# The first block's Silu through Tanh, one more VectorE operation per slice, and a new order of the instructions

## The reference

```python
qkv = jnp.einsum('bnd,ed->bne', x, W_qkv)               # x is layer-normed
attn = softmax(einsum('bnd,bmd->bnm', q * DIM**-0.5, k))
out = einsum('bnm,bmd->bnd', attn, v)
x = x + _layernorm(out)
# feed-forward on layernorm(x); _tlin(x, w, s) = (x @ w.T) * s, w is -1, 0 or 1
h = silu(_tlin(x, w1_w, w1_s)) * _tlin(x, w2_w, w2_s)   # 128 -> 512
h = gelu(_tlin(h, h1_w, h1_s))                          # 512 -> 512
h = gelu(_tlin(h, h2_w, h2_s))                          # 512 -> 512
x = x + _layernorm(_tlin(h, w3_w, w3_s))                # 512 -> 128
```

## Time and profile before

| what | us |
|---|---|
| median of 3 runs (129.56 to 130.08) | 129.98 |
| the profiled execution, its own time | 130.0 |
| its span, first to last instruction | 127.8 |
| PE busy | 122.6 |
| VectorE busy | 103.3 |
| ScalarE busy | 97.4 |
| table loads on ScalarE, up to 27 us: those at 0.75, 18.76, 23.35 and 25.69 | 4 x 1.28 |

### The profile page before, as it was taken

One profiled execution on the slowest core, in us unless ns is written; L12 is line 12 of the kernel. 1 busy time (PEld: TensorE's weight loads), 2 busy tenths in 40 slices (PEclk: granted clock), 3 DMA queues, 4 the chain that ended last, 5 costly groups with the idle time before them and its releaser, 6 DMA issues.

```text
span 127.8 us, 2356 instructions
## 1 busy us (share of the span) xinstructions
PE 122.6 (96%) x698; PEld 102.5 (80%) x698; DVE 103.3 (81%) x337; ACT 97.4 (76%) x182; POOL 27.9 (22%) x40
## 2 busy tenths in 40 slices
PE   7999999999999999999999999999999999999980
PEld 5585979989778988887889888888888788899970
DVE  0697789998898997888798998458999895695853
ACT  4248887987999739599899189799992996997520
POOL 3294220033300015230000054400001550000351
PEclk9999999999999999999999999999999999999999
DMA  4899999100000000010000000010000002000003
GB/s 106 250 308 379 381 375 373 33 5 3 0 0 5 0 5 0 3 41 0 0 5 0 0 5 0 16 68 0 8 0 0 0 5 82 0 5 0 0 29 100
DMA packets 5344, 8.28 MB, mean 65 GB/s; under 512 B 465, under 2 KB 2769, under 8 KB 5329
## 3 DMA queue, kind: packets, MB, share of 16 engines
q1 hardware_dynamic: 3840, 5.12, 12.6%
q0 software_dynamic: 1344, 2.88, 6.7%
q10 hardware_dynamic: 144, 0.07, 0.2%
HBM read 7.02 MB, written 1.05 MB: 63 GB/s over the span
## 4 chain that ended last, share of the span: by engine, by line
PE 84%; DVE 6%; DMA 3%; ACT 1%; SPq 1%; issue 1%; DVEq 0%; ACTq 0%
PE F L1181 22%; PE F L1187 22%; PE A L1090 5%; PE A L1058 5%; PE F L1130 5%; PE F L1137 5%; PE A L1187 3%; PE A L1181 3%; DMA xs<-x 3%; PE A L1041 3%; PE A L1074 2%; PE A L1029 2%; DVE xn_odd L653 2%; PE F L1210 1%; PE A L1222 1%
## 5 line engine op out<-in xcount | busy, mean ns | idle before, releaser
L319 POOL TENSOR_TENSOR rstd<-mv,minus_half 128x4 f32<-128x4 f32 (+1 forms) x19 | 17.7, 935 | 87.1 <-DVE mv L637 87.0
L1181 PE MATMUL F<-a_hi,h_hi 128*128 128x512 f32 (+1 forms) x152 | 35.5, 355 | 0.0
L630 DVE TENSOR_TENSOR a_lo<-act_full,a_hi 128x512 fp32r<-128x512 f32 (+1 forms) x52 | 30.6, 602 | 5.9 <-ACT act_full L432 5.2
L1187 PE MATMUL F<-a_lo,h_hi 128*128 128x512 f32 (+1 forms) x152 | 34.9, 352 | 0.0
L440 ACT ACTIVATE a_hi<-F,sc 128x512 fp32r<-128x512 f32 (+1 forms) x33 | 20.5, 632 | 12.2 <-PE F L1187 12.2
L1187 PEld LDWEIGHTS F<-a_lo,h_hi 128*128 128x128 f32 x152 | 25.7, 189 | 4.0
L1181 PEld LDWEIGHTS F<-a_hi,h_hi 128*128 128x128 f32 x152 | 25.2, 189 | 3.6 <-issue 0.2
L432 ACT ACTIVATE act_full<-F,sc 128x512 f32<-128x512 f32 (+1 forms) x38 | 23.1, 621 | 1.7 <-PE F L1187 1.7
L733 DVE SCALAR_TENSOR_TENSOR act_full<-F,sc,silu 128x512 f32<-128x512 f32 (+1 forms) x16 | 10.7, 676 | 1.0 <-ACT silu L421 0.8
L421 ACT ACTIVATE silu<-F,sc 128x512 f32<-128x512 f32 (+1 forms) x16 | 9.8, 633 | 1.1 <-PE F L1137 0.9
L1130 PE MATMUL F<-x2T_hi,w_hi 128*128 128x512 f32 (+1 forms) x32 | 10.3, 405 | 0.1
(11 more groups left out here) (158 smaller groups left out, 198.5 us busy)
## 6 DMA issues: line engine op xcount, KB each, us to landing
h_raw<-h SPq DMA_DIRECT2D x2, 1024.0 KB, 11.2
h_hi<-h POOLq DMA_DIRECT2D x2, 1024.0 KB, 12.1
xs<-x SPq DMA_DIRECT2D x3, 256.0 KB, 3.9
out<-outs SPq DMA_DIRECT2D x3, 256.0 KB, 2.1
w_raw<-w SPq DMA_DIRECT2D x1, 512.0 KB, 6.4
w_hi<-w POOLq DMA_DIRECT2D x1, 512.0 KB, 7.3
xs<-x SPq DMA_DIRECT2D x2, 128.0 KB, 8.9
w_raw<-w SPq DMA_DIRECT2D x1, 256.0 KB, 16.1
```

The source lines that it names most:

```text
L319: nc.gpsimd.tensor_tensor(rstd[:, ln, tiles(b)], mv[:, ln, tiles(b), 1], minus_half[:, 0:SIZES[b]], ALU.pow).then_inc(rstd_ready[ln], 1)
L630: nc.vector.tensor_tensor(dst, full, hi.bitcast(f32), ALU.subtract).then_inc(done, 1)
L1181: nc.tensor.matmul(out, terms[k][0], terms[k][2], start=(k == 0), stop=False)
L1187: last = [nc.tensor.matmul(out, terms[k][0], terms[k][3], start=False, stop=(k == KT - 1)) for out, terms in groups]
```

## The change

In block 0 alone (`BY_TANH = (0,)`) ScalarE computes t = tanh(w1_s/2 * u) where it computed Silu(w1_s * u), u being the first product in PSUM. VectorE then makes (t + 1) * u of it, in place in `silu1` (`one_and_tanh`, new, four calls of 128x256), and the gate multiplies with w1_s * w2_s / 2 in place of w2_s. The two new columns of scales, `half_w1` and `half_w12`, are made by two small VectorE instructions (`halves`). Tanh is in the table set that Exp uses.

One of the copies of block 1, `pT_copy(1, 0)`, goes from VectorE to ScalarE. The order of all engines' lists is new in many places; the numbers of instructions are otherwise as before, but for `keep_warm`, of which 6 of the 8 ahead of `x_transposes(1)` are gone, and the 2 ahead of `g_projection(0)` stand in their place.

```diff
+        half_w1, half_w12 = sb("half_w1", [P, KT]), sb("half_w12", [P, KT])
+        BY_TANH = (0,)
-        BY_DVE = ((0, 0, 0, 1, 1), (0, 0, 0, 1, 1), (0, 0, 0, 1, 1), (1, 1, 0, 1, 1, 1, 0, 1))
+        BY_DVE = ((0, 0, 0, 1, 1), (0, 0, 0, 1, 1), (0, 0, 0, 1, 1), (1, 0, 0, 1, 1, 1, 0, 1))
@@ silu
+                if b in BY_TANH:
+                    act.wait_ge(halves_ready, 2)
+                    nc.scalar.activation(silu1[:, o % 2, c], up_banks(b, o)[0][:, c], ACT.Tanh,
+                                         scale=half_w1[:, o:o + 1]).then_inc(silu_ready, 1)
+                    return
@@ vector engine
+            def halves():
+                dve.wait_ge(sc_loaded, 16)
+                nc.vector.tensor_scalar(half_w1[:, :], sc[:, S_W1:S_W1 + KT], 0.5, None, ALU.mult).then_inc(halves_ready, 1)
+                nc.vector.scalar_tensor_tensor(half_w12[:, :], sc[:, S_W1:S_W1 + KT], 0.5, sc[:, S_W2:S_W2 + KT],
+                                               ALU.mult, ALU.mult).then_inc(halves_ready, 1)
+            def one_and_tanh(b, o):
+                c = slice(0, width(b))
+                dve.wait_ge(silu_ready, KT * b + o + 1)
+                nc.vector.scalar_tensor_tensor(silu1[:, o % 2, c], silu1[:, o % 2, c], 1.0, up_banks(b, o)[0][:, c],
+                                               ALU.add, ALU.mult).then_inc(silu_product, 1)
@@ gate
+                if b in BY_TANH:
+                    dve.wait_ge(silu_product, KT * BY_TANH.index(b) + o + 1)
+                    dve.wait_ge(halves_ready, 2)
+                    w2_scale = half_w12[:, o:o + 1]
@@ order on the vector engine, first block
+            halves()
+            x2T_low(0)
             low_sum(3)
@@ order on the tensor engine, before x_transposes(1)
-            keep_warm(F[0], 8)
```

More of the change, by code:

```diff
@@ L534, in _ @@
             gelu_high(A2, 1, 1)
+            gelu_high(A2, 1, 2)
             gelu(A2, 1, 1)
-            gelu_high(A2, 1, 2)
             gelu(A2, 1, 2)
@@ L825, in _ @@
             x1_normalised(0)
+            halves()
+            x2T_low(0)
             low_sum(3)
-            x2T_low(0)
-            pT_copy(1, 0)
+            squared_sums(1)
             low_sum(4)
-            squared_sums(1)
+            one_and_tanh(0, 0)
+            one_and_tanh(0, 1)
             gate(0, 0)
@@ L833, in _ @@
             high(A1, 0, 0)
+            low_sum(5)
+            attention_out(1)
+            maxima(2, 0)
+            one_and_tanh(0, 2)
             high(A1, 0, 1)
             low(A1, 0, 0)
+            copy_flags(1)
             low(A1, 0, 1)
-            low_sum(5)
             gate(0, 2)
+            one_and_tanh(0, 3)
             high(A1, 0, 2)
-            maxima(2, 0)
+            gate(0, 3)
             low(A1, 0, 2)
-            attention_out(1)
-            gate(0, 3)
             high(A1, 0, 3)
-            copy_flags(1)
             low(A1, 0, 3)
@@ L854, in _ @@
             low(A3, 0, 0)
+            low(A3, 0, 1)
             x2T_low(1)
-            x_normalised(3)
             maxima(2, 1)
             pT_copy(2, 0)
-            low(A3, 0, 1)
+            low(A3, 0, 2)
             gate(1, 0)
             gate(1, 1)
-            low(A3, 0, 2)
             low(A3, 0, 3)
             high(A1, 1, 0)
+            x_normalised(3)
+            squared_sums(2)
             high(A1, 1, 1)
+            pT_copy(2, 1)
             low(A1, 1, 0)
-            pT_copy(2, 1)
-            squared_sums(2)
+            gate(1, 2)
             low(A1, 1, 1)
-            gate(1, 2)
             high(A1, 1, 2)
@@ L898, in _ @@
             low(A1, 2, 0)
-            low(A3, 1, 3)
             pT_copy(3, 0)
+            gate(2, 2)
             high(A1, 2, 1)
-            gate(2, 2)
             high(A1, 2, 2)
@@ L946, in _ @@
             y_shifts(2)
-            x1_normalised(4)
             low(A2, 3, 0)
             low(A2, 3, 1)
+            x1_normalised(4)
+            x2T_low(4)
             low(A2, 3, 2)
-            x2T_low(4)
-            shift_x1(4)
             low(A2, 3, 3)
@@ L955, in _ @@
             gate(4, 1)
+            gate(4, 2)
             high(A1, 4, 0)
-            gate(4, 2)
+            high(A1, 4, 1)
+            low(A1, 4, 0)
+            shift_x1(4)
             gate(4, 3)
-            low(A1, 4, 0)
-            high(A1, 4, 1)
             high(A1, 4, 2)
             low(A1, 4, 1)
-            high(A3, 3, 0)
             high(A1, 4, 3)
             low(A1, 4, 2)
+            high(A3, 3, 0)
             low(A3, 3, 0)
@@ L1237, in _ @@
             x_transposes(0)
+            g_projection(0)
+            scores(0, 0)
+            v_projection(0)
+            w3_broadcast()
             keep_warm(A[0], 2)
-            g_projection(0)
-            v_projection(0)
-            scores(0, 0)
-            w3_broadcast()
-            keep_warm(F[0], 8)
             x_transposes(1)
@@ L1249, in _ @@
             scores(1, 0)
+            scores(1, 1)
             v_projection(1)
-            scores(1, 1)
+            sum_flags(0)
             g_projection(2)
-            sum_flags(0)
+            read_flag(0)
+            probs_transposes(1, 0)
+            x2_transposes(0)
             v_projection(2)
-            read_flag(0)
-            x2_transposes(0)
-            probs_transposes(1, 0)
-            probs_transposes(1, 1)
             up_high(0, 0)
@@ L1262, in _ @@
             up_low(0, 1)
+            probs_transposes(1, 1)
             attend(1, 0)
+            attend(1, 1)
+            scores(2, 0)
             up_high(0, 2)
@@ L1345, in _ @@
             up_low(3, 2)
+            up_high(3, 3)
+            probs_transposes(4, 0)
+            up_low(3, 3)
             end(A3, 2, (0,), 3)
-            probs_transposes(4, 0)
-            up_high(3, 3)
-            up_low(3, 3)
             attend(4, 0)
```

101 lines of the change are left out of this document (52 added, 49 removed).

## The result

| | median, us | runs |
|---|---|---|
| before, beside it | 129.77 | 129.36 to 130.08 |
| changed kernel | 132.88 | 131.01, 132.26, 133.5, 133.6 |

A forecast was written before the change was run, and what follows sets the result against it. PE bounds the kernel, busy for 122.6 of 127.8 us, with VectorE nearly full in block 0's gates. 130.0 us plus 1.5, less 0.25, less 0.25, gave 131.0; range 129.1 to 132.2.

The forecast's parts named there:

- ScalarE's loads at nothing: Block 0: removing two table loads, 2.57 us of ScalarE's time, gains nothing, with 0.5 us as the other end.
- The rival with ScalarE as pace-maker: Block 0: the loads held back Silus and exps, so the kernel gets faster, 128.5 us; chance 0.15.
- VectorE's price: Block 0's gates: VectorE gets net 1.6 us more work and starts 0.1 us later, so the last low ends at 28.5.
- So VectorE decides: Block 0's h1: PE is ready at 28.1, ahead of the last low, so its matmul starts 1.5 us later (1.1 to 1.9).
- VectorE's full stretch: Sign in block 0: VectorE busy without a gap from x2T_lo at about 18.9 to the last a_lo at about 28.5.
- PE's idle time at the flag's read: Sign around 17.3: PE stands from about 17.0 to 17.6; the 0.6 us are covered by later waits.
- the products' distance of 0.40: Sign in block 0: the four one_and_tanh on VectorE stand at distances of 0.40 us.
- The pair at 107.37: Sign near the end: this pair of matmuls stands at 108.6, showing what was given back until then.
- Given back from 34 to 43, 0.25: Later PE work: waits for a copy and for block 1's gates give 0.25 us back (0 to 0.6).
- Given back near the end, 0.25: At up_high(4, 2): shift_x1(4) moved behind the gates, and lows ahead of copies, give 0.25 us back (0 to 0.5).
- The other moves are each nothing: Rest of the kernel: other moves stand where PE has no wait; each costs nothing, or 0.1 us for one.
- The rival of the clock: Whole kernel: the clock case puts the time at 132.6 us; chance 0.08.

The follow-up runs named there:

- e11_before_no_product: e4_before_tanh without the four one_and_tanh, so the product by (tanh + 1) is left out; 129.72 us, ratio 0.9995.
- e3_warm_silu: e1_warm with Silu in block 0 again and without one_and_tanh and halves, the new orders kept; 134.74 us, ratio 1.0387.
- e1_warm: The changed kernel with keep_warm as before: 2 ahead of g_projection(0), 8 ahead of x_transposes(1); 131.63 us, ratio 1.014.
- e7_no_product: e1_warm without the four one_and_tanh of VectorE, so the product by (tanh + 1) is left out of block 0; 131.68 us, ratio 1.0142.
- e12_moved: e8_late_orders with Tanh and product, pT_copy(1, 0) on ScalarE and attention_out(1) behind block 0's last low; 131.93 us, ratio 1.0186.
- e4_before_tanh: The kernel before, in its orders, with Tanh, halves and the four one_and_tanh in block 0; 131.01 us, ratio 1.0094.
- e8_late_orders: The kernel before up to block 0's end, then the changed kernel's orders with x2T_low(4) behind low(A2, 3, 2); 129.65 us, ratio 0.9987.
- e6_warm_tail: e1_warm with x2T_low(4) put behind low(A2, 3, 2), as the kernel before has it; 131.0 us, ratio 1.0087.
- e5_warm_sum: e1_warm with low_sum(3) put back ahead of x2T_low(0), as the kernel before has it; 131.74 us, ratio 1.016.
- e2_cold: The kernel before with only its keep_warm matmuls cut as in the changed kernel; 130.24 us, ratio 1.0057.

## Why the prediction was right or wrong

**ScalarE's loads at nothing: right.** e11_before_no_product has them gone in the orders of before and pays no product: ratio 0.9995. The rival with ScalarE as pace-maker, 128.5 us, falls. In the changed kernel's trace no load stands between the Tanh at 24.99 and the exps at 25.79. e3_warm_silu shows the other side, four loads of 1.28 us where the calls alternate.

**VectorE's price: right in size, by luck.** I had the stretch from 18.87 to 28.5, 9.63 us; it is 9.56. The four products took 0.33 each, not 0.40, and about 0.2 is saved where the third and fourth gate are no longer followed at once by the `high` that reads them (0.39 and 0.40 to the next operation, 0.51 and 0.48 before). Against that, a wait of 0.44 that I hadn't seen stands between the two sums. The profile shows no releaser for it ("issue"). By the code a `low_sum` waits for the `low_sum` before it (`dve.wait_ge(low_by_dve, before)`), and the change takes away the copy that stood between them; but that alone isn't the cause, since in e3_warm_silu the same two sums, with the same tiny operation between them, start 0.80 us apart (19.44 and 20.24) and leave no gap, for 1.21 here. What makes the wait is open.

**"So VectorE decides": the step that failed, though its number held.** I put PE at 28.1, "just ahead of the last `low`", 9.23 behind `x2T_lo(0)`, and took the later of the two. They are a tie: in e1_warm the last `low` ends at 9.55, and PE, without idle time from `scores(2, 1)` on, comes to the matmul at 9.72. That is 0.49 later than I had it: `scores(2, 1)` starts 0.28 later (7.11 for 6.83), and from there PE takes 2.6 us, not 2.4. e7_no_product shows PE's own limit, where `low` is 0.80 earlier and PE only 0.28. The 1.5 us are right (9.72 for 8.30 is 1.42), but half of the cause is missing: `scores(2, 1)` ahead of `begin`, which puts 2.6 us of PE's work behind the exps instead of 1.26 (8.30 - 7.04); in e12_moved, with `begin` ahead again, it is 1.17 (8.88 - 7.71), though no run moved `begin` alone. Either cause by itself costs it nearly all: e4_before_tanh has only VectorE's (c 9.95), e7_no_product only PE's (c 9.44). Their prices don't add, and undoing one gives next to nothing back.

**What was to be seen.** Of the marks that the prediction named, ScalarE's one load, VectorE's full stretch (but for the 0.44) and PE's idle time at the flag's read (0.27 us for 0.6) and ahead of `scores(2, 1)` are there; the products' distance of 0.40 is not. `gelu_high(A2, 0, 0)` was to come at 28.9, 10.03 us behind `x2T_lo(0)`; it comes at 29.87, also 10.03 behind it. The pair at 107.37 was to stand at 108.6 and stands at 110.15, in e1_warm at 108.97: less was given back than forecast.

**Given back from 34 to 43, 0.25: the cause came, and most of it was lost again.** In e1_warm PE's delay against before is 1.19 us at block 1's first `up_high` (35.10 for 33.91) and 0.93 at `attend(2, 0)` (37.78 for 36.85), behind the copy that is no longer late: 0.26 as I said. But the next four matmuls, for which I named the wait for block 1's gates, are 1.13 late (39.07 for 37.94), and so is block 1's h1 (44.16 for 43.03). e8_late_orders shows the same two steps; e4_before_tanh, with the old orders, is 1.69, 1.70 and 1.69 late at these three places and gives nothing back. By the first matmuls of block 3's h2 (102.44 before) e1_warm is 1.01 late, e4_before_tanh 1.57.

**Given back near the end, 0.25: wrong in sign.** In e1_warm the delay grows from 1.01 to 1.48 us at the last matmul. I read the pair at 107.37, whose wait does go, and not what the same new order does to the queue ahead of it, `low(A2, 3, 2)` behind `x2T_low(4)`. e6_warm_tail shows its price, 0.53 us in the trace. This term, 0.25 less forecast and 0.5 more measured, is about what e1_warm's 131.63 lies above the forecast.

**"The other moves are each nothing": wrong. The clock: its time met in one execution, its term in none.** The rival of the clock, 132.6 us, to which I gave 0.08, was an estimate of mine, 1.6 us above the forecast, and no run shows that term; what the profiled execution, 132.26, shows in its place is 0.94 us at a lower granted clock. Its start is 1.2 us behind e1_warm's (`x2T_lo(0)` 19.84 for 18.62), and two rows make that up: `xT_copy(0)` 0.27 later (5.78 for 5.51) behind `w3_diagonal`, and 2.07 - 1.13 = 0.94 for `scores(0, 0)` at the lower clock. The trace of before has 1.00 in the three stretches from 6 to 12 us, this one 0.77, 0.50 and 0.88, and PE had stood for 0.76 and 0.47 us there. That these gaps did it isn't shown: in e5_warm_sum PE stood for 1.06 us at the same place, and 0.47 behind it, and the clock stayed at 1.00.

Nor is it shown that the cut of `keep_warm` is needed for the fall. One of the changed kernel's four runs has it (0.985 over the span) and none of e1_warm's five, but e3_warm_silu, with the matmuls back, shows 0.987 in three of six, and e2_cold, without them, 0.995 or more in all twelve. That `w3_diagonal`'s wait is what turns the scale wasn't tried: no run undid that move alone. In the earlier trace rows a `keep_warm` matmul takes 0.22 us in the first group and 0.13 in the last; the granted clock is 1.00 in both stretches (0.78 to 3.71 and 8.46 to 9.52), so it is not what sets them apart, and what does is open.

So the sum goes: 129.8 before, about 1.2 for the two causes in block 0 (after what is given back), 0.5 to 0.6 for the wait near the end: 131.6, as in e1_warm. The profiled execution of the changed kernel has about 1 us more for its start; the run of 131.01, with a granted clock of 0.997 over its span, can't have had as much of it.

## What to carry to other kernels

Where two chains end within 0.2 us of each other (9.55 and 9.72 in e1_warm), pricing one isn't enough: a new cost on either is real, and a gain on one alone is not (e7_no_product: 0.80 less on VectorE, 0.28 less on PE). Of a reordering, read every moved instruction for what it waits for, at its new place, and for what is queued behind it; here a copy behind a transfer and a `low` behind an x2T cost 0.3 and 0.5 us, and neither showed in the totals. Cutting instructions whose result nobody reads can cost time: 0.4 us in the kernel before (e2_cold), for a reason that is open. And one profile is one execution: this one had a granted clock of 0.985 over its span, and no other of its kernel's four runs was below 0.997.

## What I had not expected of the hardware

- Two `one_and_tanh` of 128x256, independent of each other, start 0.33 us apart in the changed kernel (22.01 to 22.67 for two); where the gate that reads the result follows at once, the distance is 0.45 (e4_before_tanh: 20.44 to 20.89).
- Idle time of 0.44 us that the profile puts to "issue" comes back in six of the traces at the same place, and is gone in e3_warm_silu with the same order of these instructions but for `halves` and the products; its cause is open.
- The granted clock fell to 0.50 after gaps of 0.76 and 0.47 us on PE (changed kernel), and stayed at 1.00 after gaps of 1.06 and 0.47 (e5_warm_sum).
- The copy that waits for the transfer of the scales, 8.5 KB, started at 4.74 us in one execution (e7_no_product), at 5.47 in the changed kernel's and at 6.07 in e5_warm_sum's; from issue to landing the transfer took 2.6, 3.3 and 3.9 us in the three.
